# Leaving out fifteen matmuls on a matrix of ones at the start of a one-core macaron kernel

## Chip, core and metric

The kernel runs on one core of a Trainium2 chip. The metric is the device time of one execution in microseconds (us), the median over several executions. TensorE appears in the profile as PE (matmuls) and PEld (weight loads), VectorE as DVE, ScalarE as ACT, GpSimd as POOL, SyncE as SP.

## The reference

`x` is 4 x 1024 tokens of 128 channels in float32. Three half layers are applied to it: a mixture-of-experts layer, a linear attention, and the same mixture-of-experts layer again.

```python
x = x + 0.5 * ffn(layernorm(x))
x = x + attn(layernorm(x))
x = x + 0.5 * ffn(layernorm(x))

def ffn(x):                                  # 16 experts, 2 shared experts, F = D = 128
    combine = top4_of_top2_groups(sigmoid(x @ router_w.T) + bias)      # [tokens, 16]
    y = silu(x @ gate_w[e]) * (x @ up_w[e]) @ down_w[e]                # all experts, dense
    return (combine * y).sum(over experts) + silu(x @ sh_gate_w) * (x @ sh_up_w) @ sh_down_w
def attn(x):                                 # 32 heads of 4 channels, no softmax
    a = einsum('bthd,bshd->bhts', q, k); ctx = einsum('bhts,bshd->bthd', a, v)
    return groupnorm(ctx) @ out_w.T + out_b
```

## The kernel before

The 4096 tokens are cut into 8 blocks of 512. A *step* is one mixture-of-experts layer on one block, so there are 16 steps, and two steps make a *pair*. Within a step the kernel goes through 18 *units* (2 shared experts and 16 routed ones). A unit has three products of 128x128 weights with 128x512 activations: gate, up and down. Each is done to nearly float32 precision as three matmuls in float32r (`product`, L447 to L451): high part by high part (L449), low part of the weights by high part (L450), high part by low part of the activations (L451). A record of these three lines of 128x512 in the profile is one such matmul.

The order of the work is written out by hand on each engine, with semaphores between the engines. Around a unit it goes like this:

- PE: gate product into `gateP`, up product into `upP` (in the first step other banks too, `first_up`), and four units later the down product into `yP`.
- ACT: silu of `gateP` (L840), and the high part `A_hi` of the gated activation (L814). In the first step it also rounds the weights to their high part `W_hi` (`split_high`, L718), in an order given by the table `HIGH_AT`: units 0 to 2 ahead of the first silu, unit 3 after silu 0, units 4 and 5 after silu 1, units 6 to 9 after silu 3, and then one after each of later silus.
- DVE: the routing weights (`CB`) by the silu (L1137), times the up product, which gives `A` (L1168); also the layer norm's statistics and the routing.
- POOL: the low part of the weights `W_lo` (`split_low`, L333) in the first step, and in every unit the low part `A_lo` of the activations (L340), for which the down product waits.
- SP: all DMA.

The first step begins with a chain through all engines: the block of `x` is loaded, DVE and POOL work out the statistics, DVE normalises it into `XN` (L1202), PE transposes it (`transpose_next`, L480), DVE copies the result to `XT` (L1221), PE multiplies it with the router's weights (`logits`, L488), while ACT and DVE split `XT` into `XT_hi` (L747) and `XT_lo` (L1230). Then PE does the first units in the order gate 0, up 0, gate 1, up 1, gate 2, gate 3, up 2, up 3, gate 4 (`first_units`), 3 matmuls each.

PE's own program begins, ahead of the pairs, with these lines; `WARM` is 13 and `FILL` is 2:

```python
def keep_busy(count):
    for _ in range(count):
        pe.matmul(yP[:, 0:P], ones[:, :], ones[:, :], start=True, stop=True)
...
pe.wait_ge(const_seq, IDENT_AT)
keep_busy(WARM)
pe.wait_ge(router_in, 16)
pe.transpose(attP[:, 3 * P:3 * P + E], R_in[:, :], ident[0:E, 0:E]).then_inc(setup_psum, 1)
keep_busy(FILL)
transpose_next(0)
```

Nothing reads what these fifteen matmuls write to `yP`: the first real product there starts with `start=True`. Each of them is in float32 and stands in the profile as two records of 128x128.

Of the kernel before, what the change touches and what calls it, by code (L numbers as in the profile page):

```python
# [48 lines left out]
def macaron_kernel(nc, x, Wqkv_w, Wqkv_b, gn_w, gn_b, out_w, out_b, router_w, bias,  # L49
# [14 lines left out]
    ESEM = 4  # L64
    CSEM = 2
    SPREAD = 4
    WARM, FILL = 13, 2
    ROUTE_OPS = 22
    CONSTS = 10
    IDENT_AT = 4  # L70
# [1216 lines left out]
```

## Time and profile before

| what | value |
|---|---|
| median of 3 runs | 670.13 us (669.88 to 670.77) |
| the profiled execution's own time | 671.6 us |
| its span, first to last instruction | 669.9 us |
| PE busy | 661.1 us (99%) |
| DVE, POOL, ACT busy | 522.3, 446.5, 406.4 us |
| mean granted clock of PE | 0.995 |

The profile is of one execution, whose own time is 1.5 us above the median of the others; the span lacks the 1.7 us that lie around the first and the last instruction. The times in the rows below are counted from the start of the span. A granted clock of 1.00 stands for 2.4 GHz and one of 0.50 for 1.2 GHz. Matmuls are pipelined, so a record's duration is longer than the distance to the next record's start; that distance is the cost of one in a row of many. Where a row holds several records (x4), its time runs from the first start to the last end.

### The profile page before, as it was taken

What the parts mean: (1) busy time and instruction counts of PE and PEld (TensorE: products, weight loads), DVE (VectorE), ACT (ScalarE), POOL (GpSimd) and SP (SyncE); (2) the same over time, 40 slices, a digit from 0 to 9 for tenths busy, and PEclk for the clock granted to TensorE, in tenths of its full rate; (3) what the DMA queues carried; (4) which work ended last, traced back from release to release, by engine and by line L of the source; (5) the groups of instructions that cost most, each with busy time, mean ns of one, the idle gap of its engine ahead of it and who ended that gap; (6) DMA issues with size and microseconds to landing.
All of it is one profiled execution on the core that took longest, in us unless ns stands there. A gap on an engine that the chain in (4) does not pass through costs nothing.

```text
span 669.9 us, 10547 instructions
## 1 busy us (share of the span) xinstructions
PE 661.1 (99%) x3165; PEld 551.2 (82%) x3165; DVE 522.3 (78%) x1440; ACT 406.4 (61%) x817; POOL 446.5 (67%) x386
## 2 busy tenths in 40 slices
PE   7989999999999999999999999999999999999997
PEld 6868888888888888888888888888888888888886
DVE  6796969778687886878868778687795978868664
ACT  4856565565676556765657656676656565655554
POOL 6996666666756677666676666766667666666663
PEclk8999999999999999999999999999999999999999
DMA  9715170320506015060160510703306033150700
GB/s 232 264 58 201 54 252 2 139 114 27 226 2 234 20 45 211 0 221 33 26 229 1 199 55 17 252 1 134 136 12 259 0 131 139 46 225 0 270 0 32
DMA packets 30262, 75.38 MB, mean 113 GB/s; under 512 B 3569, under 2 KB 12545, under 8 KB 30209
## 3 DMA queue, kind: packets, MB, share of 16 engines
q1 hardware_dynamic: 30208, 74.74, 31.0%
q8 instruction: 25, 0.41, 0.2%
q14 instruction: 29, 0.23, 0.1%
HBM read 72.11 MB, written 2.62 MB: 112 GB/s over the span
## 4 chain that ended last, share of the span: by engine, by line
PE 96%; DVE 1%; DMA 1%; SPq 0%; POOL 0%; issue 0%; ACT 0%; DVEq 0%
PE gateP L449 10%; PE yP L451 10%; PE yP L449 10%; PE gateP L451 10%; PE gateP L450 10%; PE upP L451 10%; PE yP L450 10%; PE upP L449 10%; PE upP L450 10%; PE prepP L488 2%; PE attP L505 1%; PE backP L469 1%; PE prepP L480 1%; DMA W_in<-in_L_ffn_sh_down_w_dram 1%; PE attP L561 1%; PE backP L561 1%
## 5 line engine op out<-in xcount | busy, mean ns | idle before, releaser
L340 POOL TENSOR_TENSOR A_lo<-A,A_hi 128x512 fp32r<-128x512 f32 x287 | 370.6, 1293 | 205.2 <-ACT A_hi L814 205.2
L840 ACT ACTIVATE gateP<-gateP 128x512 f32<-128x512 f32 x252 | 146.6, 582 | 203.6 <-PE gateP L451 202.7
L1137 DVE TENSOR_TENSOR T<-gateP,CB 128x512 f32<-128x512 f32 x252 | 173.3, 688 | 89.1 <-ACT gateP L840 84.8
L814 ACT CAST A_hi<-A 128x512 fp32r<-128x512 f32 x287 | 176.0, 613 | 12.4 <-DVE A L1168 9.5
L1168 DVE TENSOR_TENSOR A<-upP,T 128x512 f32<-128x512 f32 x254 | 175.6, 691 | 8.7
L449 PE MATMUL gateP<-XT_hi,W_hi 128*128 128x512 f32 x288 | 119.1, 414 | 2.1 <-DVE T L1137 1.7
L449 PE MATMUL yP<-A_hi,W_hi 128*128 128x512 f32 x288 | 113.5, 394 | 0.0
L451 PE MATMUL yP<-A_lo,W_hi 128*128 128x512 f32 x288 | 112.9, 392 | 0.0
L451 PE MATMUL gateP<-XT_lo,W_hi 128*128 128x512 f32 x288 | 112.8, 392 | 0.0
L450 PE MATMUL gateP<-XT_hi,W_lo 128*128 128x512 f32 x288 | 112.7, 391 | 0.0
L450 PE MATMUL yP<-A_hi,W_lo 128*128 128x512 f32 x288 | 112.3, 390 | 0.0
L451 PE MATMUL upP<-XT_lo,W_hi 128*128 128x512 f32 (+1 forms) x286 | 112.1, 392 | 0.0
L449 PE MATMUL upP<-XT_hi,W_hi 128*128 128x512 f32 (+1 forms) x286 | 112.1, 392 | 0.0
L450 PE MATMUL upP<-XT_hi,W_lo 128*128 128x512 f32 (+1 forms) x286 | 111.8, 391 | 0.0
L449 PEld LDWEIGHTS yP<-A_hi,W_hi 128*128 128x128 f32 x288 | 54.2, 188 | 13.2 <-POOL A_lo L340 1.9
L451 PEld LDWEIGHTS gateP<-XT_lo,W_hi 128*128 128x128 f32 x288 | 54.3, 189 | 11.8
L449 PEld LDWEIGHTS gateP<-XT_hi,W_hi 128*128 128x128 f32 x288 | 54.7, 190 | 11.2 <-issue 2.1
L451 PEld LDWEIGHTS yP<-A_lo,W_hi 128*128 128x128 f32 x288 | 54.2, 188 | 11.7
L451 PEld LDWEIGHTS upP<-XT_lo,W_hi 128*128 128x128 f32 x286 | 54.1, 189 | 11.7
L450 PEld LDWEIGHTS upP<-XT_hi,W_lo 128*128 128x128 f32 x286 | 54.0, 189 | 11.6
L449 PEld LDWEIGHTS upP<-XT_hi,W_hi 128*128 128x128 f32 x286 | 53.9, 188 | 11.7
L450 PEld LDWEIGHTS yP<-A_hi,W_lo 128*128 128x128 f32 x288 | 54.2, 188 | 11.0
(223 smaller groups left out, 647.0 us busy)
## 6 DMA issues: line engine op xcount, KB each, us to landing
CB<-combT SPq DMA_DIRECT2D x126, 512.0 KB, 6.9
out_dram<-X SPq DMA_DIRECT2D x7, 256.0 KB, 2.0
X<-in_L_attn_x_dram SPq DMA_DIRECT2D x3, 512.0 KB, 9.8
W_in<-in_L_ffn_gate_w_dram SPq DMA_DIRECT2D x4, 256.0 KB, 5.2
W_in<-in_L_ffn_up_w_dram SPq DMA_DIRECT2D x4, 256.0 KB, 5.3
W_in<-in_L_ffn_down_w_dram SPq DMA_DIRECT2D x4, 256.0 KB, 5.4
X<-in_L_attn_x_dram SPq DMA_DIRECT2D x2, 256.0 KB, 3.1
combT<-CT SPq DMA_DIRECT2D x16, 32.0 KB, 1.8
```

Source lines behind the costliest of these rows:

```text
L340: pool.tensor_tensor(A_lo[:, slot, :], A[:, slot, :], A_hi[:, slot, :].bitcast(F32), ALU.subtract).then_inc(low_done, 1)
L449: pe.matmul(dst, hi_w, hi_x, start=start, stop=False)
L450: pe.matmul(dst, lo_w, hi_x, start=False, stop=False)
L451: return pe.matmul(dst, hi_w, lo_x, start=False, stop=stop)
L469: mm = pe.transpose(backP[:, j * P:(j + 1) * P], YT[:, j * P:(j + 1) * P], ident[:, :])
L480: mm = pe.transpose(prepP[:, j * P:(j + 1) * P], XN[:, j, :], ident[:, :])
L488: mm = pe.matmul(bank[:, j * E:(j + 1) * E], XT[:, j * P:(j + 1) * P], RT[:, :], start=True, stop=True)
L561: mm = pe.matmul(bank[:, j * P:(j + 1) * P], XAT[:, g * TILES + j, :], Bm[:, :], start=True, stop=True)
L814: act.copy(A_hi[:, v % SLOTS, :], A[:, v % SLOTS, :]).then_inc(high_done, 1)
L840: act.activation(dst, gateP[u % 2][:, :], ACT.Silu).then_inc(silu_done, 1)
L1137: dve.tensor_tensor(T[:, u % TS, :], silu, weights, ALU.mult).then_inc(gate_weighted, 1)
L1168: dve.tensor_tensor(A[:, u % SLOTS, :], bank[:, :], gated, ALU.mult).then_inc(mul_done, 1)
```

## The change

The two counts are set to zero, so that `keep_busy` issues nothing. The instructions around it, the waits among them, are the same.

```diff
@@ -64,7 +64,7 @@
     CSEM = 2
     SPREAD = 4
-    WARM, FILL = 13, 2
+    WARM, FILL = 0, 0
     ROUTE_OPS = 22
```

On PE this is what the start of the program turns into (its first rows; `ones` is the 128x128 matrix of ones, `R_in` the router's weights, `XN` the normalised block and `RT` the transposed router's weights):

```order
@@ -1,6 +1,4 @@
 L445 UNCONDITIONAL_BRANCH
-L576 MATMUL yP<-ones 128x128 x13
 L690 MATMUL attP<-ident,R_in 128x16
-L576 MATMUL yP<-ones 128x128 x2
 L480 MATMUL prepP<-ident,XN 128x128 x4
 L488 MATMUL backP<-RT,XT 128x16 x4
```

Thirteen matmuls ahead of the transpose of the router's weights and two behind it are gone; nothing changes place, and the rows of the other four engines are the same in both kernels.

## Rows read from the trace of the kernel before

**Rows 1.** The page: busy time by engine, and the clock in 40 slices.

```profile
PE 661.1 (99%) x3165; PEld 551.2 (82%) x3165; DVE 522.3 (78%) x1440; ACT 406.4 (61%) x817; POOL 446.5 (67%) x386
...
PEclk8999999999999999999999999999999999999999
```

**Rows 2.** PE's timeline, start of the program; last, the transposes that touch 8.10:8.15.

```profile
1.77 4.58 PE L576 MATMUL yP<-ones 128*128 128x128 f32 x26 [1.77 <-POOL ident L367]
6.28 0.23 PE L690 MATMUL attP<-ident,R_in 16*128 16x16 f32 x1
6.44 0.71 PE L576 MATMUL yP<-ones 128*128 128x128 f32 x4
7.67 0.66 PE L480 MATMUL prepP<-ident,XN 128*128 128x128 f32 x4 [0.52 <-DVE XN L1202]
9.21 1.03 PE L488 MATMUL backP<-RT,XT 128*128 128x16 f32 x8 [0.88 <-DVE XT L1221]
10.59 0.47 PE L449 MATMUL gateP<-XT_hi,W_hi 128*128 128x512 f32 x1 [0.34 <-POOL W_lo L333]
...
7.84 0.49 PE L480 MATMUL prepP<-ident,XN 128*128 128x128 f32 x3
```

**Rows 3.** PE's timeline, records that touch 3.2:3.5, 4.4:4.7, 4.7:5.0 and 5.3:5.6.

```profile
2.79 1.06 PE L576 MATMUL yP<-ones 128*128 128x128 f32 x4
...
4.07 0.83 PE L576 MATMUL yP<-ones 128*128 128x128 f32 x3
...
4.49 0.74 PE L576 MATMUL yP<-ones 128*128 128x128 f32 x4
...
5.07 0.72 PE L576 MATMUL yP<-ones 128*128 128x128 f32 x5
```

**Rows 4.** Busy time of PE (records) in stretches, then clock, DMA share, GB/s.

```profile
7.15:10.50 3.35, 1.70 (x13) 1.00 1.15 312
10.60:11.58 0.98, 0.98 (x5) 1.00 1.20 292
11.58:15.00 3.42, 3.42 (x10) 0.50 1.21 290
15.00:18.40 3.40, 3.40 (x16) 1.00 1.17 319
...
46.70:48.40 1.70, 0.00 (x0) 1.00 0.00 0
48.40:49.13 0.73, 0.72 (x3) 1.00 0.00 0
49.13:52.54 3.41, 3.41 (x9) 0.50 0.02 5
52.54:56.00 3.46, 3.46 (x19) 1.00 0.04 9
```

**Rows 5.** PE's timeline: gate 1's last record, gate 3's last record, and around them.

```profile
12.84 0.63 PE L450 MATMUL gateP<-XT_hi,W_lo 128*128 128x512 f32 x1
13.27 0.63 PE L451 MATMUL gateP<-XT_lo,W_hi 128*128 128x512 f32 x1
...
15.92 0.39 PE L450 MATMUL gateP<-XT_hi,W_lo 128*128 128x512 f32 x1
16.14 0.39 PE L451 MATMUL gateP<-XT_lo,W_hi 128*128 128x512 f32 x1
```

**Rows 6.** DVE's timeline, from the normalised block to the router's first result.

```profile
6.52 1.10 DVE L1202 TENSOR_SCALAR XN<-X,nmean,rstd 128x128 f32<-128x128 f32 x4
...
8.37 0.69 DVE L1221 COPY XT<-prepP 128x512 f32<-128x512 f32 x1 [0.26 <-PE prepP L480]
...
9.75 0.69 DVE L1230 TENSOR_TENSOR XT_lo<-prepP,XT_hi 128x512 fp32r<-128x512 f32 x1 [0.43 <-ACT XT_hi L747]
```

**Rows 7.** ACT's timeline, from silu 1 to the high part of unit 6's weights.

```profile
13.93 0.60 ACT L840 ACTIVATE S<-gateP 128x512 f32<-128x512 f32 x1 [1.38 <-PE gateP L451]
14.43 0.92 ACT L718 CAST W_hi<-W_in 128x384 fp32r<-128x384 f32 x2
15.88 1.29 ACT L840 ACTIVATE T<-gateP 128x512 f32<-128x512 f32 x2 [0.54 <-PE gateP L451]
17.07 1.74 ACT L718 CAST W_hi<-W_in 128x384 fp32r<-128x384 f32 x4
```

**Rows 8.** POOL's timeline from units 4 and 5; its last four rows ahead of the next wait.

```profile
15.00 1.99 POOL L333 TENSOR_TENSOR W_lo<-W_in,W_hi 128x384 fp32r<-128x384 f32 x2 [1.27 <-ACT W_hi L718]
17.65 3.94 POOL L333 TENSOR_TENSOR W_lo<-W_in,W_hi 128x384 fp32r<-128x384 f32 x4 [0.66 <-ACT W_hi L718]
21.53 3.81 POOL L340 TENSOR_TENSOR A_lo<-A,A_hi 128x512 fp32r<-128x512 f32 x3
...
43.35 1.06 POOL L333 TENSOR_TENSOR W_lo<-W_in,W_hi 128x384 fp32r<-128x384 f32 x1
44.33 2.59 POOL L340 TENSOR_TENSOR A_lo<-A,A_hi 128x512 fp32r<-128x512 f32 x2
47.71 1.01 POOL L351 TENSOR_TENSOR rstd<-vareps,half 128x4 f32<-128x4 f32 x1 [0.80 <-DVE vareps L912]
```

**Rows 9.** The timeline at the end of that stretch, DVE and then PE.

```profile
43.52 3.42 DVE L903 TENSOR_TENSOR parts<-bst 128x4 f32<-128x4 f32 x1
...
48.41 0.47 PE L449 MATMUL gateP<-XT_hi,W_hi 128*128 128x512 f32 x1 [1.73 <-DVE T L1137]
```

## The prediction

> **What bounds the kernel now.** I read the page first: PE is busy for 661.1 of 669.9 us [rows 1], so after its start the kernel is one long stream of matmuls, and what is lost or won on PE early is carried to the end unless another engine is the bound for a while. Then I read the stream's start, where all of the change lies. PE does 26 records on ones from 1.77 us, one small transpose, 4 more records on ones until 7.15, then it is mostly waiting: 4 records of transposes at 7.67 for `XN`, 8 of logits at 9.21 for `XT`, and the first product at 10.59 [rows 2]. The matmuls on ones delay nothing: they end at 7.15, and the transposes behind them wait for DVE's `XN`, which ends at 7.62 [rows 2, 6]. So their removal as work is worth 0. What is left is what they do to the clock.
>
> The clock must be read twice. The column says 1.00 from the start, but the same 128x128 records on ones start 0.21 us apart at 3.2 us and 0.11 us apart at 5.3 us: four of them take 1.06, which is three distances of 0.21 and the last record's own 0.42, and five take 0.72, four distances of 0.11 and 0.28 [rows 3]. Three still take 0.83 from 4.07, and four only 0.74 from 4.49. So PE starts at the lower of its two levels (1.2 GHz), is at the higher one (2.4 GHz) from about 4.7 us, and the column's 1.00 ahead of that is not to be believed. The Trainium skill ("TensorE: Matmul & The Clock Gate", Part 1) calls the throttled level the default, which activity releases; by that rule, the spacing in the trace agrees and the column does not.
>
> The level falls to 0.50 from 11.58 to 15.00 and again from 49.13 to 52.54, where PE does 10 and 9 records instead of 16 to 19 [rows 4]. Before the first fall PE had worked little (1.70 us of 7.15 to 10.50 shows it as busy, much of it the tails of short records); before the second it stood still from 46.7 to 48.4 [rows 4, 9]. So the fifteen matmuls buy the high level from 4.7 to 11.58 us and no longer. What runs in that time and matters: the transposes, the logits, and the first four to five records of products. The rest of the first units runs at the low level already today.
>
> A third reading tells whether a late PE is late at the end. POOL works without a gap from 17.65 (the low part of unit 6's weights, which waited for ACT's high part) to 46.92 (44.33 + 2.59) [rows 8]. DVE then stands in one small instruction, 43.52 to 46.94, that ends only when POOL's run ends, and PE's gap up to 48.41 waits for DVE's next product [rows 9]. So the chain of the first step is: PE's first products, ACT, POOL's unbroken 29.3 us, DVE, PE. The delay that counts is that of POOL's row at 17.65; what PE loses after gate 3 up to about 46 us is hidden behind POOL as long as it stays small.
>
> **The change, part by part.** The work taken away: 0, as above. The transpose of the router's weights can go earlier, and who waits for it (ACT's `RT`, needed at 9.21) doesn't gain, since the logits wait for `XT`. The two waits that stay cost nothing. Everything else is the same instructions at the low level, until the clock rises. Low-level prices: 0.21 us for a 128x128 record in place of 0.11 [rows 3], and 0.43 us for a 128x512 record (12.84 to 13.27) in place of 0.23 (15.92 to 16.14) [rows 5].
>
> 1. Transposes. They start at 7.67 as before (DVE's chain is untouched). At the high level they end at 8.33. At the low level: the later three starts come some 0.38 later in all (the first distance, 7.67 to 7.84, doubled, and the next two 0.21 instead of 0.11), and the last takes 0.42 instead of 0.27: the end is near 8.86, **+0.5**. `XT`, `XT_hi` and `XT_lo` hang on it with fixed durations, so `XT_lo` ends at 10.44 + 0.5 = 10.94 [rows 6].
> 2. Logits. They start at 9.21 + 0.5 = 9.7. Their eight records start 0.11 us apart ((1.03 - 0.26) / 7) [rows 2]; each has a 128-column weight load, like the records on ones, and no row shows such a short matmul at the low level. Lower bound: no change, the last starts at 10.5 and gate 0 waits for `XT_lo`, at 11.1. Upper bound: doubled to 0.21, the last starts at 11.2 and gate 0 at 11.4. I take the upper one, because the equal spacing of both kinds at the high level points to the weight load as the price. Gate 0 then starts at **11.4 in place of 10.59, +0.8** (+0.5 by the lower bound). The routing chain becomes 1.3 us late; what waits for it is PE's spreading of the weights after gate 4, where PE itself comes later too, so I cost it at nothing.
> 3. First products, until the clock rises. Nothing in the trace of before shows when it will, so it is bounded. PE's work started at 1.77 and the level rose near 4.7, 2.9 us later; products started at 10.59 and it rose at 15.00, 4.4 later; PE restarted at 48.41 and it rose at 52.54, 4.1 later [rows 2 to 4, 9]. Counted from gate 0 at 11.4 that gives 14.3 to 15.8, counted from the logits at 9.7 (the least) 12.6. I take 15.0, the moment of before, inside these.
> 4. To POOL. Gate 1's last record is the ninth: 11.4 + 8 x 0.427 = 14.8, in place of 13.27, so +1.5. Silu 1 starts at 15.45 (13.93 + 1.5). Behind it on ACT stand the high parts of units 4 and 5 (0.50 after it, 0.92 long), silus 2 and 3, then unit 6's high part 1.19 after those start. Before, 0.54 us of ACT's time there was a wait for gate 2 [rows 7], and that slack is now used: 15.45 + 0.50 + 0.92 = 16.87 for silu 2, and 18.06 for unit 6, in place of 17.07: **+1.0**. Gate 3 does not decide: its last record is the eighteenth, (15.0 - 11.4) / 0.427 = 8.4 records are low and 8.6 more cost 0.229 each, so it starts at 17.0 and ends at 17.4, when silu 2 is just ending.
> 5. POOL. Units 4 and 5 begin at 15.00 + 1.5 and end at 18.5; unit 6 begins at 17.65 + 1.0 = 18.65. Its run and everything behind it move by 1.0.
>
> The sum is 0 + 1.0: 671.6 + 1.0 = 672.6 for a profiled execution like that of before, and 1.0 over the median of 670.13: **671.1 us**, 0.15% longer. Fifteen matmuls of 4.58 + 0.71 us are taken away and the time hardly moves, and rather up.
>
> **The rivals.** By "no change" I mean within 0.2%, or 1.34 us, about what a measurement can tell.
>
> - *The clock rises later* (slower). If the rise comes after 15.8, gate 3 takes over from gate 1 as what sets unit 6. At a rise at 15.9 its last record starts at 17.4 and ends at 17.8, and with a silu (0.6) unit 6 is at 18.4: +1.3, which is the point from which it decides. At 17.6 the last record ends at 18.6: +2.1. With the low level all through, at 11.4 + 17 x 0.427 + 0.63 = 19.3: +2.7. So 671.5 to 672.8. For it: the three distances of step 3 differ by 1.5 us, and the three runs of before lie 0.9 us apart, so something moves between executions. Against it: 15.8 lies behind all the distances counted from gate 0. The Trainium skill ("TensorE: Matmul & The Clock Gate", Part 1) says that the transition depends on where the activity monitor's own time stands when the kernel starts, so the moment varies by run; one trace can't show that. Chance 0.30.
> - *The clock rises early, or the logits aren't slowed* (no change). Rise at 12.6 to 12.8: gate 1's last record starts near 14.1, silu 2 near 16.0, unit 6 at 17.2: +0.1. The same comes out, 0, if the start's 1.00 in the clock column were true. For it: the logits' weight loads keep PE busy from 9.7. Against it: before, 1.0 us of logits and 1.0 us of products ahead of 11.58 did not keep the level up [rows 4]. 670.1 to 670.5, chance 0.15.
> - *The second low stretch goes away* (a gain elsewhere). It costs some eight records (9 instead of 17), 8 x 0.229 = 1.8 us. PE's gap of 1.7 us moves by 1.0, and may then no longer lead to a fall. 670.13 + 1.0 - 1.8 = 669.3; chance 0.08. Together with an early rise it would be 668.4, the only way that I see to more than 0.2% faster; chance 0.04.
> - *The forecast*, +0.4 to +1.3: chance 0.43.
>
> **How the numbers follow.** Predicted 671.1. No change: 0.43 + 0.15 + 0.08 = 0.66; slower 0.30; faster 0.04. The range runs from 669.5, near the vanished second stretch, to 672.4, a late rise near 17.6; what is left out is the last 0.04, about half of the 0.08 and a low level beyond 17.6, under 0.15 in all.
>
> **What the profile of after would show.** Right: no records on ones; transposes starting at 7.67 and ending near 8.9; logits over some 1.9 us; gate 0 near 11.4; the first products 0.43 us apart from the very first one, up to a rise near 15; silu 1 near 15.5; POOL's unbroken run starting near 18.65 and ending near 47.9; PE's wait for DVE still there; one low stretch near 50. Wrong: gate 0 at 11.1 or less (step 2); a rise before 14 or after 15.8 (step 3), visible as the place where the spacing turns from 0.43 to 0.23; a POOL run that starts with the same delay but has gaps, so that PE is what counts (step 4); no low stretch near 50, or a second one after it.

## The result and the profile after

The changed kernel takes 672.89 us (median of 5, 671.98 to 673.29) beside 670.13 for the kernel before: a ratio of 1.0038, with a 95% interval of 1.0023 to 1.0053, so 1.5 to 3.6 us slower. Twelve more executions of it gave 672.67. The forecast of 671.1 had the direction right, and both its size and the upper end of its range, 672.4, were too low.

The profiled execution alone would mislead. Its span is 670.5 us, 0.6 over that of before, and its mean granted clock is 0.999, above the 0.995 of before. Both are accounted for below.

PE's timeline of the changed kernel, at the places of [rows 2] and [rows 5] (start, duration, line, record, wait before it):

```profile
3.85 0.25 PE L690 MATMUL attP<-ident,R_in 16*128 16x16 f32 x1 [3.85 <-DMA R_in<-in_L_ffn_router_w_dram]
7.72 1.12 PE L480 MATMUL prepP<-ident,XN 128*128 128x128 f32 x4 [3.62 <-DVE XN L1202]
9.71 1.86 PE L488 MATMUL backP<-RT,XT 128*128 128x16 f32 x8 [0.87 <-DVE XT L1221]
11.41 0.77 PE L449 MATMUL gateP<-XT_hi,W_hi 128*128 128x512 f32 x1
...
14.97 0.63 PE L451 MATMUL gateP<-XT_lo,W_hi 128*128 128x512 f32 x1
...
17.11 0.47 PE L450 MATMUL gateP<-XT_hi,W_lo 128*128 128x512 f32 x1
17.41 0.40 PE L451 MATMUL gateP<-XT_lo,W_hi 128*128 128x512 f32 x1
...
18.11 0.39 PE L451 MATMUL gateP<-XT_lo,W_hi 128*128 128x512 f32 x1
```

Transposes and logits take 1.12 and 1.86 us where they took 0.66 and 1.03, and gate 0 starts at 11.41 instead of 10.59. Gate 1's last record starts at 14.97 (13.27 before) and gate 3's at 18.11 (16.14 before). The distance between starts turns from 0.43 to 0.23 only at about 17.2. ACT hands this to POOL:

```profile
15.64 0.60 ACT L840 ACTIVATE S<-gateP 128x512 f32<-128x512 f32 x1 [1.56 <-PE gateP L451]
16.13 0.92 ACT L718 CAST W_hi<-W_in 128x384 fp32r<-128x384 f32 x2
17.84 1.29 ACT L840 ACTIVATE T<-gateP 128x512 f32<-128x512 f32 x2 [0.80 <-PE gateP L451]
19.03 1.74 ACT L718 CAST W_hi<-W_in 128x384 fp32r<-128x384 f32 x4
```

```profile
16.71 1.99 POOL L333 TENSOR_TENSOR W_lo<-W_in,W_hi 128x384 fp32r<-128x384 f32 x2 [1.55 <-ACT W_hi L718]
19.61 3.95 POOL L333 TENSOR_TENSOR W_lo<-W_in,W_hi 128x384 fp32r<-128x384 f32 x4 [0.91 <-ACT W_hi L718]
...
46.29 2.58 POOL L340 TENSOR_TENSOR A_lo<-A,A_hi 128x512 fp32r<-128x512 f32 x2
49.67 1.01 POOL L351 TENSOR_TENSOR rstd<-vareps,half 128x4 f32<-128x4 f32 x1 [0.80 <-DVE vareps L912]
```

POOL's unbroken run starts at 19.61 in place of 17.65, +1.96, and the row behind it at 49.67 in place of 47.71, again +1.96 [rows 8]. DVE's wait and PE's gap move with it:

```profile
45.48 3.42 DVE L903 TENSOR_TENSOR parts<-bst 128x4 f32<-128x4 f32 x1
...
50.37 0.47 PE L449 MATMUL gateP<-XT_hi,W_hi 128*128 128x512 f32 x1 [1.71 <-DVE T L1137]
```

PE restarts at 50.37 in place of 48.41 [rows 9]. From there this one execution wins back 1.4 of its 1.96 us (its span is only 0.6 us longer): here the wait near 48 us is not followed by a *low stretch*, a time in which the granted clock is 0.50, 1.2 GHz (49.13 to 52.54 us before [rows 4]). In stretches (length, PE busy with its records, clock, DMA share, GB/s), the kernel after in 48 to 52 and 52 to 56:

```profile
48.00:52.00 4.00, 2.29 (x10) 1.00 0.00 0
52.00:56.00 4.00, 4.00 (x21) 1.00 0.00 0
```

and the same kernel in another execution, of the last run below, whose span is 671.0; there the low stretch follows:

```profile
48.00:52.00 4.00, 2.34 (x6) 0.73 0.00 0
52.00:56.00 4.00, 4.00 (x19) 0.84 0.02 4
```

### The profile page after: what moved, and what is told of

Read it like the earlier page. It is cut to its first block, busy times and chain, and to the rows that moved or that the text cites. A ratio compares the mean times of both kernels' runs of the same rounds, so it can differ in the third digit from the quotient of the medians.

```text
span 670.5 us, 10488 instructions
## 1 busy us (share of the span) xinstructions
PE 656.8 (98%) x3135; PEld 547.0 (82%) x3135; DVE 521.8 (78%) x1440; ACT 407.2 (61%) x817; POOL 446.5 (67%) x386
## 4 chain that ended last, share of the span: by engine, by line
PE 97%; DVE 2%; DMA 1%; SPq 0%; issue 0%; DVEq 0%; ACT 0%
PE gateP L449 10%; PE gateP L451 10%; PE gateP L450 10%; PE yP L451 10%; PE yP L449 10%; PE upP L449 10%; PE upP L451 10%; PE yP L450 10%; PE upP L450 10%; PE prepP L488 2%; PE prepP L480 1%; PE attP L505 1%; PE backP L469 1%; PE attP L561 1%; PE backP L561 1%; DMA X<-in_L_attn_x_dram 1%
```

## The experiments

Each was run against the kernel before, in some 12 executions unless it says otherwise. Where an execution's mean granted clock is given, it is for the whole span, in which one low stretch takes off 0.0025 (half of its length in the rows before, 3.4 us, over 670); 0.999 is a low level at the very end of the span, where PE's work is nearly done. The *first* low stretch is the one near 12 us, the *second* the one near 50.

**The kernel before, repeated.** No edit.

> The kernel before once more, unchanged, for the spread of its executions and the granted clock of each. Theory (the low level of the clock comes in none, one or two later stretches, and this moves the time): the executions fall into groups 1.0 to 1.5 us apart, with clocks of 0.995, 0.997 and above 0.999, and the lowest clock goes with the longest time; median within 0.5 us of 670.1. Rival (the spread is noise of DMA or start): times 1 us apart with the same clock.

With the kernel before's executions beside this run and the later ones, 110 in all:

```
mean clock      executions   us (lowest to highest)   low stretches, by the clock
1.0             19           668.46 to 668.75         none
0.996, 0.997    81           669.84 to 670.90         one
0.995           10           671.45 to 671.68         two
```

The theory holds: each stretch costs some 1.5 us. The number of stretches is worked out from the mean clock, and seen in a timeline only where an execution was profiled. The profile that the prediction was made from (671.6 us, 0.995) is of the third kind, with two stretches; so is this run's (671.68). What most executions do had not been in front of me.

**The fifteen, each on one column.** They stay as instructions and keep the array hardly busy.

```diff
-pe.matmul(yP[:, 0:P], ones[:, :], ones[:, :], start=True, stop=True)
+pe.matmul(yP[0:1, 0:1], ones[:, 0:1], ones[:, 0:1], start=True, stop=True)
```

> The fifteen matmuls stay, as many instructions at the same places, but each works on one column of weights and one column of data. Theory (what counts is that the array is busy, which raises the clock): it behaves like the kernel without them, low level until about 17 us, POOL's unbroken run from about 19.6 us, 672.9 us. Rival (what counts is that the instructions stand there, for instance because PE's program is fetched earlier or its first matmuls are slow): like before, 670.1 us, POOL's run from 17.65 us.

672.63 us, ratio 1.0031 (1.0020 to 1.0042), and the rest of the timeline is that of the changed kernel, with POOL's unbroken run from 19.44:

```profile
1.78 0.79 PE L576 MATMUL yP<-ones 128*1 128x1 f32 x26 [1.78 <-POOL ident L367]
...
7.66 1.12 PE L480 MATMUL prepP<-ident,XN 128*128 128x128 f32 x4 [3.50 <-DVE XN L1202]
9.65 1.86 PE L488 MATMUL backP<-RT,XT 128*128 128x16 f32 x8 [0.87 <-DVE XT L1221]
11.35 0.77 PE L449 MATMUL gateP<-XT_hi,W_hi 128*128 128x512 f32 x1
```

The median is 2.4 us above that of before and not told from the changed kernel's (672.67). So the instructions alone do nothing that can be measured; what counts is the work that they put on the array.

**More matmuls in PE's gaps** (fill 4 instead of 2, and four and two more):

```diff
-    WARM, FILL = 13, 2
+    WARM, FILL = 13, 4
...
 transpose_next(0)
+keep_busy(4)
 pe.wait_ge(setup_sb, 1)
 logits(0)
+keep_busy(2)
```

> The kernel before with 8 more matmuls on ones: 2 more ahead of the transposes of the first block, 4 between them and the logits, 2 behind the logits, so that PE stands still for less than 0.3 us between 1.8 and 10.6 us. Theory: the level, raised at about 4.7 us, doesn't fall near 10 to 12 us, the first products come every 0.23 us, POOL's run starts at about 16.9 us instead of 17.65, and the median is 0.7 us or more below that of before. Rival (the fall follows from something else than PE's idleness, or the first units are bound by DMA and ACT): no difference, within 0.3 us.

669.84 us, ratio 0.9994 (0.9980 to 1.0008): not told from the kernel before. Six executions lie at 668.52 to 669.10 (clock 1.0) and six at 670.58 to 671.02 (0.997). In the trace the first stretch is gone (20 records in 11 to 15 us at a clock of 1.00, 13 at 0.57 before), but the level first rose late in that execution, the 26 records on ones took 5.62 us instead of 4.58, and the transposes started at 8.48 instead of 7.67. What the filling won was partly lost to that delay. The median says nothing for or against the filling. That the first stretch is missing fits the theory, but it is one trace, and by their clock many executions of later runs lack that stretch though nothing was filled in at the start.

**The changed kernel, with PE's later gap filled.** Seven matmuls on ones ahead of gate 16, where PE waits for DVE; `keep_busy` takes the bank as a second argument.

```diff
+if first and u == 16 and i == 0:
+    keep_busy(7, attP)
```

> The changed kernel, without the fifteen, with 7 matmuls on ones in PE's wait of 1.7 us at about 48 us (ahead of the gate product of the seventeenth unit in program order, into the bank attP that nothing uses then). Theory (part of the changed kernel's executions have a low stretch near 50 us, which costs 1.0 us or more): all executions at a clock of 0.999, the median 671.9 to 672.1, 0.9 us under that of the changed kernel. Rival (the stretch costs nothing at the end): the same median as the changed kernel, 672.9.

671.12 us (670.75 to 672.23), no execution below a clock of 0.999. That is 1.6 us under the changed kernel's 672.67, more than the 0.9 I expected: all twelve are at 672.23 or less, where seven of twelve were above 672.5. The gap is filled (PE's timeline):

```profile
47.15 1.72 PE L576 MATMUL attP<-ones 128*128 128x128 f32 x14
48.93 0.50 PE L449 MATMUL gateP<-XT_hi,W_hi 128*128 128x512 f32 x1
```

**The kernel before, with the same filling.**

> The kernel before, with the fifteen, and 7 more matmuls on ones in PE's wait at about 47 us, as in the fourth run. Theory (before, two of three executions have one low stretch, and it is the one near 49 us): the second stretch goes, the median falls to 668.7, and against the changed kernel with the same filling (671.1) the fifteen are worth 2.4 us. Rival (the one stretch of most executions is the first, near 11 us): the median stays at 670.2.

668.72 us, ratio 0.9990 (0.9977 to 1.0002), so by the interval just not told from the kernel before; the groups say more. Seven executions are at 668.44 to 668.78 (clock 0.999 and 1.0) and five at 670.09 to 670.50 (0.996 and 0.997). One of the five was profiled, and its stretch is the first, near 11.5:

```profile
11.52 0.58 PE L450 MATMUL upP<-XT_hi,W_lo 128*128 128x512 f32 x1
11.90 0.63 PE L451 MATMUL upP<-XT_lo,W_hi 128*128 128x512 f32 x1
```

So both halves were partly right: the second stretch is frequent, and without it the median is 1.3 us lower (670.03 - 668.72). One stretch is left in 5 of 12 executions and costs 1.6 us; in the profiled one it is the first, and I take it to be the first in the other four. Against the changed kernel with the same filling, the fifteen are worth 671.12 - 668.72 = 2.40 us in the median.

**Six instead of thirteen** (`WARM, FILL = 6, 2`).

> Six matmuls on ones instead of thirteen ahead of the router's transpose, and the two behind it. Theory (the level must have been raised by them before it can help, and six end near 4.4 us): it rises in few executions or not at all, median 672.0 to 672.9, near the changed kernel. Rival (any start helps in proportion): half of the way, 671.5.

670.87 us, ratio 1.0025 (1.0012 to 1.0037), with single executions up to 673.2. This is lower than both expected. The one that was profiled (672.60, clock 0.992) is of a kind that 3 of 12 show; seven lie at 670.63 to 670.89. In it the logits take 1.76 us, the level having fallen again ahead of them, and POOL's run starts at 18.66. My theory, that six could hardly raise the level, is wrong: even there the transposes took 0.66 us, the duration of the high level.

**Eight right ahead of the transposes, none before** (`WARM, FILL = 0, 8`).

> None ahead of the router's transpose, eight behind it, so that PE works on ones from about 3.9 to at least 7.3 us, right up to the first transposes. Theory (work close to the first transposes raises the level at 7 to 8 us and it is less likely to fall by 11): as good as before or a little better, 669.5 to 670.3. Rival (the level is raised too late for the transposes and logits): 671 to 672.

670.57 us (668.96 to 672.01), ratio 1.0005 (0.9992 to 1.0017). Three executions at 669.0, seven at 670.1 to 670.7, two at 671.6 and 672.0: the groups of before, some 0.4 us later. The median lies between the theory and the rival. In the trace the transposes are still slow (1.12 us) and the logits fast again (1.04 us), with gate 0 at 11.05.

**Statistics by way of PSUM.** The third block's statistics, in the first step, as the kernel already does it for the second block: a reduction and intermediate values in `attP`.

```diff
+if isinstance(t, int) and t == 2:
+    dve.tensor_reduce(s2, b2, AX.X, ALU.add).then_inc(stats_seq, 1)      # s2, d2, w2 lie in attP
+    ...
+    dve.scalar_tensor_tensor(dst, bst[:, :, 1], 2.0, s2[:, :, 0], ALU.mult, ALU.subtract)
+    ...
+    return
 merge_stats(stats_seq, 4 * t, bst, nmean[:, :], vareps[:, :], parts)
```

> The kernel before, with the statistics of the third block, which DVE works out in the thirteenth unit of the first step, written by a reduction with its intermediate values in the bank attP, as the kernel does it for the second block, in place of operations with two inputs in SBUF. Theory (DVE's small operation stands until POOL's unbroken run ends, and PE's gap of 1.7 us and the second low stretch follow from it): the 3.4 us operation is gone, PE's gap falls below 0.5 us, no low stretch near 49 us, median 668.0 or less. Rival (POOL's run itself holds PE back there): the gap stays, 670.2.

666.80 us, ratio 0.9961 (0.9949 to 0.9974), faster than the kernel before. DVE's small operation, 3.42 us long while POOL ran [rows 9], is now

```profile
43.98 0.16 DVE L948 TENSOR_REDUCE attP<-bst 128x8 f32<-128x16 f32 x1
44.18 0.16 DVE L951 SCALAR_TENSOR_TENSOR parts<-bst,attP 128x4 f32<-128x4 f32 x1
```

while POOL works beside it without a break, and PE has no wait between 15 and 60 us. In the kernel before the next operation of the same form (L904), which started when POOL's run had ended, took 0.15 us:

```profile
46.86 0.15 DVE L904 TENSOR_TENSOR parts<-bst 128x4 f32<-128x4 f32 x1
```

Four of 11 executions are at 668.45 to 668.79 with one low stretch, which is the first in the profiled one; the others are at 666.50 to 666.83. This profile (668.72 us) shows something else of the start, with the same fifteen matmuls as before:

```profile
1.77 5.88 PE L576 MATMUL yP<-ones 128*128 128x128 f32 x26 [1.77 <-POOL ident L367]
8.30 0.60 PE L480 MATMUL prepP<-ident,XN 128*128 128x128 f32 x4
```

The level rose later here, the matmuls on ones took 5.88 us instead of 4.58, and the transposes started at 8.30 instead of 7.67, without a wait for `XN`. In such an execution the fifteen delay PE by some 0.6 us.

**The same, without the fifteen.**

> The statistics through attP as in the eighth run, and none of the fifteen. Theory (the fifteen are worth the early delay alone, 1.5 to 2.5 us by the moment at which the clock rises, and that passes to the end undiminished): 666.8 + 2.4 = 669.2, all executions between 668.1 and 670.0. Rival (part of the 2.5 us came by way of the wait near 49 us and its low stretch): under 668.3.

669.50 us (668.66 to 670.16). Without any gap near 48 us the fifteen are worth 669.50 - 666.80 = 2.70 us. That is no less than with the gap (2.40 and some 2.6), so no part of their worth is seen to come by way of the second stretch. The two profiled executions, this one (669.28) and the one above with the first stretch (668.72), are only 0.6 us apart.

**The same, with the gaps at the start filled** (`WARM, FILL = 12, 2`, four behind the transposes, two behind the logits).

> The statistics through attP, twelve matmuls on ones ahead of the router's transpose, two behind it, four between the first transposes and the logits, two behind the logits. Theory (both low stretches are gone, and what differs between executions is only when the level first rises): all executions at a clock of 0.999 or more and between 666.3 and 667.2, median 666.6, so hardly below the eighth run's median but without its third of executions at 668.7. Rival (the matmuls in the gaps delay the chain of the first block): 667.3 or more.

Six executions: 666.64 us (666.51 to 666.96), ratio 0.9950 (0.9936 to 0.9963), all at a clock of 0.999 or 1.0. It is the lowest median of the study, but not told from the eighth run's (666.80). It is level with the good executions of that run and lacks the group at 668.7. In its trace, as in the third run's, the first stretch is gone: 19 records in 11 to 15 us at a clock of 1.00. Seven of 11 executions were good without the filling, so six of six are a sign that it removes the first stretch, not a proof.

**The thirteen without the two** (`WARM, FILL = 13, 0`).

> The thirteen stay, the two behind the router's transpose go. Theory (the two add 0.4 us of work close to the first transposes, a small part): 670.1 to 670.8, with a few more executions that have the first low stretch. Rival (the two are what holds the level up): like the changed kernel, over 672.

670.03 us, ratio 0.9996 (0.9983 to 1.0009), five executions at 668.48 to 668.65, three at 671.22 to 671.82. In the profiled one (670.24, clock 0.997) the one low stretch is the first. The two behind the router's transpose bring nothing that can be measured.

**The changed kernel, repeated.** No edit.

> The changed kernel once more, unchanged, for more executions. Theory (no execution can be good, since the first products run at the low level in all; the moment of the rise, 14.4 to 17.6 us, and the stretch near 50 us make the spread): none below 670.7, groups near 671.0, 672.1 and 673.0, median 672.6 to 672.9. Rival (the first five executions were an unlucky draw): a median near 671.5 and some at 670.

672.67 us, none below 670.68: three at 670.68 to 670.98 (clock 1.0), two at 672.0 to 672.1 (0.999), seven at 672.57 to 673.24 (0.997). PE's and POOL's timelines of the profiled one, which took 672.78 us:

```profile
15.76 0.40 PE L450 MATMUL upP<-XT_hi,W_lo 128*128 128x512 f32 x1
...
18.89 3.95 POOL L333 TENSOR_TENSOR W_lo<-W_in,W_hi 128x384 fp32r<-128x384 f32 x4 [0.22 <-ACT W_hi L718]
```

## Why the prediction was wrong

**What bounds the kernel, and the way of the delay: right.** POOL's unbroken run, DVE's wait and PE's gap all moved by the same 1.96 us in the first trace. In the second POOL's run moved by 1.24 (17.65 to 18.89) and PE's restart by 1.25 (48.41 to 49.66). The way by POOL isn't the only one, though: in the kernels without DVE's wait PE has no gap, its own stream carries the delay, and the fifteen were worth as much (2.70 us).

**The work taken away, 0: right for the profiled execution, not for all.** Where the level rises late, as in the eighth run's profile, the matmuls on ones end behind `XN` and delay the transposes by 0.6 us.

**Steps 1 and 2, transposes and logits: right.** Forecast to end near 8.86 and to take 1.9 us; measured 8.84 (7.72 + 1.12) and 1.86. The logits do double, and gate 0 came at 11.41 for a forecast 11.4.

**Step 3, the moment of the rise: too early in most traces, and not one moment.** I took 15.0. By the spacing of the products it was about 17.2 and 15.7 in the two traces of the changed kernel, 16.9 in the run with the matmuls on one column, 15.2 without the fifteen and without DVE's wait, and 14.4 in the changed kernel with the later gap filled. The rival "the clock rises later" describes the first trace: it gave +2.1 for 17.6, and +1.96 was measured at 17.2. At 15.7 it was +1.24, where step 4's working gives about +1.2. The moment seems to be worth 1.2 us of the whole time: of the executions of the changed kernel without a stretch near 50 us, three took 670.7 to 671.0 (clock 1.0) and four 672.0 to 672.2 (0.999), and the profiled ones at 0.999 are those that rose at 17.2 and 16.9. The others of these groups have no profile.

**The step that failed: "the fifteen matmuls buy the high level from 4.7 to 11.58 us and no longer", and with it the +1.0 that the sum puts on the median.** That is so in the profiled execution. With the later gap filled, 5 of 12 executions of the kernel before had a low stretch left (670.09 to 670.50). In the other seven (668.44 to 668.78) the mean clock leaves no room for one, so the level stayed up through the first products; of such an execution without added matmuls there is no profile. Against the 671.12 of the changed kernel so filled, the fifteen are worth 0.9 us where the stretch is there, close to the 1.0 that I worked out, and 2.5 where it isn't. The median of that run is of the second kind. In the unfilled kernels the forecast was +1.0 and the medians differ by 2.8 (672.89 - 670.13), or 2.6 in the last round (672.67 against 670.09). The kernel before has two low stretches that it can be without, and 100 of its 110 executions lack at least one. The changed kernel can be without the second only, since its first products run at the low level in every trace. My sum started from an execution of before that had both (10 of 110), worked out the small loss against that, and carried it to a median that had lost one of them.

A median jumps from one group to the next, so its differences overstate a little. By means, the fifteen are worth 2.3 us (672.38 of 17 executions against 670.11 of 110), 2.0 with the later gap filled and 2.1 with the statistics by way of PSUM.

**The same, seen from the whole time.** For a profiled execution like that of before I forecast 672.6. The second profiled execution of the changed kernel, with the stretch near 50 us as before, took 672.78, and the ten of its kind 672.57 to 673.29. The working was about right for its own base, with some luck in the rise at 15.7; the move to 670.13 was not. The front of this document had the warning: the profiled execution lay 1.5 us above the median, which is one low stretch.

**The other rivals.** "The clock rises early": no execution of the changed kernel was below 670.68. "The second low stretch goes away": it did in the first trace and, by the clock, in 7 of 17 executions, but the kernel before lacks it often too, so no gain is left in the median. I costed it at 1.8 us, and the groups of before lie 1.6 apart (668.6 and 670.2). Two sums of the rivals are slightly off and change nothing: with a rise at 12.6 to 12.8 gate 1's last record starts near 13.9, not 14.1, and the low level all through gives +2.8, not +2.7.

What decides whether an execution has a given stretch I can't show from inside the kernel. The Trainium skill ("TensorE: Matmul & The Clock Gate", Part 1) says that the transition's moment depends on where the monitor's own time stands at the first matmul. The moments from 14.4 to 17.2 us behind the same instructions agree with a moment that varies; what they depend on no run here shows.

**Left open.** How the 81 executions of the kernel before with one stretch divide between the first and the second is not counted; the kernels with the gap filled or gone (5 of 12 and 4 of 11 with one stretch left) suggest that both are frequent. Why six matmuls came out at 670.9, 1.8 us lower than the changed kernel, is open: its only trace is of a slower kind than most of its executions. That filling the first waits removes the first stretch rests on two traces and six executions.

## What to carry to other kernels

Before putting a difference worked out in one trace on a median, see of what kind that execution was: where its time is off the median by as much as one event in it costs, the event may be missing from most executions, and each kind has its own sum. Work whose result nobody reads can pay, if it raises PE's clock ahead of the first products. Here thirteen such matmuls from 1.8 us did; six brought most of it, eight right ahead of the transposes did about as well (670.57 us, not told from the kernel before), and the last two of the fifteen added nothing. Filling the waits between the first real instructions too may help, but its gain was not clear of the noise; taking away the wait further on gave the most. Look at the spacing of equal matmuls, not at the mean clock: the profiled execution of the changed kernel shows 0.999 against 0.995, and the changed kernel is the slower one.

## What the runs showed of the hardware that I had not expected

The clock column of this profile begins with 1.00 and stays there until the first recorded change, though 128x512 records in the changed kernel start 0.43 us apart up to 17.2 us. All of the time at the low level ahead of the first rise is missing from the mean.

PE's wait of 1.7 us near 48 us is enough for a low stretch to follow in some executions, and not in others: of the two traces of the changed kernel one has it and one hasn't, and with the wait filled in that kernel no execution's clock is below 0.999.

DVE's operation on 128x4 elements with two inputs in SBUF took 3.42 us while POOL worked without a break, over more than one POOL instruction, and ended with POOL's run. The same form took 0.15 us once POOL had stopped, and with one of the inputs in PSUM its replacement took 0.16 us while POOL worked. The Trainium skill ("SBUF — State Buffer", section "Who interferes with whom") says that a DVE instruction with two SBUF inputs contends with a GpSimd instruction that reads SBUF, because the two engines share one pair of ports, which is held for a whole instruction. In this trace the wait was longer than that: it lasted through the rest of one and two further instructions of POOL [rows 8, 9]. Avoiding that one wait gave 3.2 us in the median (670.03 - 666.80). Of this 2.0 us is the wait itself, as between executions without a low stretch (668.6 and 666.6), and the rest comes of the second low stretch, which no longer follows. Together it is more than the fifteen matmuls are worth.
